# Turning a unit's running maxima head by head: two places in a two-slot PSUM ring, and two VectorE row-maximum operations

## The chip, the cores and the metric

One core of one Trainium2 chip runs the whole program. The metric is the device time of one execution in microseconds (us). The kernel before takes 1535.57 us, the median of two runs (1534.63 and 1536.50).

## What is computed

The reference takes 8 graphs of 1500 nodes with 64 features, and one 0/1 adjacency matrix per graph. Each graph goes through a masked graph attention with 4 heads (16 features in and out per head), then three propagations over the same adjacency, and after each of the four a residual and a layer norm over the features:

```
masked = a * scores
masked = where(masked >= 0, masked, 0.2 * masked) / sqrt(16)
attn   = softmax(masked + (-1e9 where a == 0)) * (a != 0)
x = layernorm(x + relu(attn @ feats + bias))
x = layernorm(x + (adj + I) @ x / rowsum(adj + I))
x = layernorm(x + (adj @ (x @ w2) + bias2))
x = layernorm(x + where(adj @ x > 0.5, 1, 0 * (adj @ x)))
```

## The kernel before, in words

The attention is cut into 48 **units**: 8 graphs, 2 pairs of heads, 3 slices of 500 nodes. A unit has 12 **steps**, and a step q (0 to 575) handles 125 neighbours against the slice's 500 nodes for both heads of the pair. So a graph is 72 steps, and a step's place in its graph is r = q mod 72. The other three layers of the graph before are spread over the same steps.

What a step passes through:

- TensorE fills Z (`fill_z`, L599 and L601): for each of the two heads one matmul with the mask and one with the scores. Z is a ring with two slots (RZ = 2), each of two PSUM banks of 500 columns, one for each head.
- ScalarE empties the slot with a leaky ReLU into a row buffer LS (`bend`, L774), 126x1000 in one operation.
- VectorE folds the row into the running maxima RP (`maximum`, L914 and L920), and in the unit's last step writes them to RUN (L918).
- Once the unit is folded, TensorE turns RUN into a ring slot (`turn_run`, L612, 8 transposes, 4 for each head), VectorE reduces the slot to the maxima of each node (`row_maxima`, L926, LMAX), SyncE writes LMAX to memory and reads it back broadcast to all partitions as MB (`spread_maxima`, L413 and L419).
- 19 steps after its fill, GpSimd (two of three rows, L533) or VectorE (every third, L934) subtracts MB from the row; 21 steps after it ScalarE takes the exponential (`expo`, L782), and 23 steps after it TensorE weighs the features with it (`weigh`, L628, for two steps together).
- At the unit's end the sums are turned into a ring slot as well (`turn_sums`, L637, and `keep`, L948 to L960).

The other layers use a bank M1 for their products (`collect`, L683), a ring slot for turning them back (`turn_back`, L697), and VectorE, ScalarE and GpSimd for adding, squares, powers and scaling (L983 to L1024, L828, L832, L538, L542). `power` and `low` on GpSimd are written for HALVES parts in the changed kernel; with HALVES = 1 they do what they did.

The order on every engine is written out by hand. Each engine runs its own loop over q, and tables say in which steps of a unit or a graph something stands: TURNED for turning the maxima on TensorE, MAXIMA for reducing them on VectorE, SPREAD for SyncE. For the six units of a graph TURNED puts the turning at r = 15, 27, 38, 51, 63 and 75 (the last is r = 3 of the next graph), behind the fill of that step. I call these the **six places**; they are units 24 to 29 in the fifth graph, for instance. The turning of the last unit stands at LAST_RT = 576.

Who may use a ring slot when is set by a list, `ring`, of everything that goes through Z in order. `ring_free` looks at the entry two before: a fill must have been bent, a turning reduced (`max_found`), a turned sum kept, a turned-back layer added. With one entry for the turning, the entries around it and their waits are

```
Z(q)   RT(u)              Z(q+1)          Z(q+2)
       waits bend(q-1)    waits bend(q)   waits max_found of u
```

Of the kernel before, what the change touches and what calls it, by code (L numbers as in the profile page):

```python
# [6 lines left out]
B, N, F = 8, 1500, 64  # L7
H, D = 4, 16
P = 125
# [33 lines left out]
POOL_AT, SUB_AT, EXP_AT, WEIGH_AT = 19, 19, 21, 23  # L43
LAG = POOL_AT

TURNED = (15, 15, 14, 15, 15, 15)
MAXIMA = (15, 15, 14, 14, 15, 14)
SPREAD = (16, 16, 16, 15, 15, 15)
TAKE = (35, 35, 35, 34, 34, 34)
SUMS = (36, 36, 36, 36, 35, 35)  # L50
# [2 lines left out]
CENTRE = (25, 45, 67, 86)  # L53
SQUARE = (26, 47, 66, 87)
SUM = (26, 46, 66, 88)
POWER = (28, 49, 66, 89)
SCALE = (28, 49, 67, 90)
HIGH = (29, 51, 69)
LOW = (30, 50, 70)
# [12 lines left out]
FEATURES = (14, 18, 19, 20, 22, 23, 27, 30, 32)  # L72
TAKEN = (14, 18, 19, 20, 22, 24, 27, 30, 32)
LOWER = (17, 23, 29)
KINDS = tuple((kind, c) for c in range(NS) for kind in ("XT", "FT", "FE"))
LOWER_KINDS = tuple(("FT", c) for c in range(NS))
LOADS = (57, 55, 60, 59, 65, 62, 66, 68, 30, 35, 37, 38)
# [23 lines left out]
def adj_resnorm(nc, x, adj, wv, wself, wother, bias0, w2, bias2, out):  # L101
# [13 lines left out]
    with ctx:  # L115
# [197 lines left out]
        for q in range(END):  # L313
            if q < QN:
                ring.append(("Z", q))
            if rows_at(q, BACK):
                ring.append(("W", *rows_at(q, BACK)))
            if turned_at(q, TURNED, LAST_RT) is not None:
                ring.append(("RT", turned_at(q, TURNED, LAST_RT)))
            if unit_at(q, SUMS) is not None:  # L320
                ring.append(("G", unit_at(q, SUMS)))
# [41 lines left out]
        def _(sp):  # L363
# [40 lines left out]
                             ).then_inc(at_in[slot], 16)  # L404

            def spread_maxima(u):
                sp.wait_ge(max_found, u + 1)
                if u >= 2:

                    sp.wait_ge(mb_in[u % 2], 16 * (u // 2))  # L410

                for rows in (slice(0, 112), slice(112, P)):
                    sp.dma_start(spread[u % 2].rearrange("(h i c) -> i h c", i=P, c=ST)[rows],  # L413
                                 LMAX[rows, u % 2, :].rearrange("p (h c) -> p h c", c=ST)).then_inc(max_out[u % 2], 16)
                sp.wait_ge(max_out[u % 2], 32 * (u // 2 + 1))
# [52 lines left out]
        def _(pool):  # L468
# [66 lines left out]
            def power(b, l):  # L535

                pool.wait_ge(var_ok, 4 * b + l + 1)
                nc.gpsimd.tensor_tensor(RSTD[:, :], RSTD[:, :], NHALF[:, :], ALU.pow).then_inc(rstd_ok, 1)  # L538

            def low(b, l):  # L540
                pool.wait_ge(xh_ready, 3 * b + l + 1)
                nc.gpsimd.tensor_tensor(XP[:, :, F:2 * F], X[:, :, :], XP[:, :, 0:F], ALU.subtract).then_inc(xp_ready, 1)  # L542

            for q in range(END):
                if layer_at(q, LOW):
                    low(*layer_at(q, LOW))
                if layer_at(q, POWER):
                    power(*layer_at(q, POWER))
# [17 lines left out]
        def _(pe):  # L566
            def ring_free(n):

                if n < RZ:
                    return  # L570
                kind, *at = ring[n - RZ]
                if kind == "Z":
                    pe.wait_ge(bent, at[0] + 1)
                elif kind == "RT":
                    pe.wait_ge(max_found, at[0] + 1)
                elif kind == "G":
                    pe.wait_ge(kept_seq, 5 * at[0] + 5)
                else:
                    b, l, c = at
                    pe.wait_ge(added, 9 * b + 3 * l + c + 1)  # L580
# [21 lines left out]
                                            FS[:, p, s * C:(s + 1) * C], start=False, stop=True)  # L602
                last.then_inc(z_full, 1)

            def turn_run(u):

                pe.wait_ge(maxed, STEPS * (u + 1))
                ring_free(place["RT", u])
                z = banks("RT", u)
                for hh in range(2):  # L610
                    for c in range(ST):
                        last = nc.tensor.transpose(z[:P, hh, c * P:(c + 1) * P], RUN[:, u % 2, hh, c:C:ST], ID[:P, :P])  # L612
                last.then_inc(run_turned, 1)

            def weigh(w):
# [62 lines left out]
            def collect(b, l, c, part):  # L678
                if part == 0:
                    m1_free(order["Y", b, l, c])  # L680
                    pe.wait_ge(xp_ready, 3 * b + l + 1)
# [39 lines left out]
            for q in range(END):  # L721
# [11 lines left out]
                e = q - WEIGH_AT  # L733
                if 0 <= e < QN and e % 2:
                    weigh(e // 2)
                u = turned_at(q, TURNED, LAST_RT)
                if u is not None:
                    turn_run(u)


            pe.wait_ge(kept_seq, 5 * NU)
# [151 lines left out]
        def _(dve):  # L893
# [13 lines left out]
            def maximum(q):  # L907
# [5 lines left out]
                if m == 0:  # L913
                    nc.vector.tensor_scalar(run, rows, FLOOR, None, ALU.max).then_inc(maxed, 1)  # L914
                elif m == STEPS - 1:
                    if u >= 2:
                        dve.wait_ge(run_turned, u - 1)
                    nc.vector.tensor_tensor(RUN[:, u % 2, :, :], rows, run, ALU.max).then_inc(maxed, 1)  # L918
                else:
                    nc.vector.tensor_tensor(run, rows, run, ALU.max).then_inc(maxed, 1)  # L920

            def row_maxima(u):
                dve.wait_ge(run_turned, u + 1)
                if u >= 2:
                    dve.wait_ge(max_out[u % 2], 32 * (u // 2))
                nc.vector.tensor_reduce(LMAX[:, u % 2, :].rearrange("p (h c) -> p h c", c=ST),  # L926
                                        banks("RT", u)[:P].rearrange("p h (c m) -> p h c m", c=ST),
                                        AX.X, ALU.max).then_inc(max_found, 1)

            def subtract(e):  # L930
# [65 lines left out]
            def scale(b, l):  # L996

                dve.wait_ge(m1_read, order["S", b, l])
                dve.wait_ge(rstd_ok, 4 * b + l + 1)
# [108 lines left out]
            for q in range(END):  # L1108
# [7 lines left out]
                u = turned_at(q, MAXIMA, LAST_RT)  # L1116
                if u is not None:
                    row_maxima(u)
# [69 lines left out]
```

## Time and profile before

| | |
|---|---|
| median of two runs | 1535.57 us |
| the profiled execution | 1531.98 us, of which the span of the core's instructions is 1529.9 us |
| TensorE busy | 1343.7 us, 88% of the span |
| VectorE busy | 1266.8 us, 83% |
| ScalarE busy | 1223.3 us, 80% |
| GpSimd busy | 1035.5 us, 68% |
| mean granted TensorE clock | 0.946 of full speed |

Columns of the rows below: a group of instructions is "line engine operation out<-in (shape) xcount", its busy time and the mean ns of one, and then the engine's idle time just before them with what ended most of it. In a timeline a row is "start, us it takes, engine line operation xcount", and square brackets tell the idle time before it and what ended it. A row of a timeline may cover several instructions in a row, and the start of the next can lie before its end, since operations are pipelined. PE is TensorE, PEld its weight loads, DVE VectorE, ACT ScalarE, POOL GpSimd and SP SyncE.

### The profile page before, as it was taken

Reading aid. Unit: us, or ns where it says so; the run is one execution under the profiler, and the core shown is the slowest. Engines: PE = TensorE matmul, PEld = TensorE weight load, DVE = VectorE, ACT = ScalarE, POOL = GpSimd, SP = SyncE. Lnnn points to the kernel's source line nnn. Section 1 sums busy time; section 2 is a strip of 40 time slices with the busy share of each in tenths; the row PEclk is TensorE's granted clock in tenths of the full one; section 3 lists DMA queues with packets and bytes.
Section 4 is the critical chain, followed back from the end, with each engine's and each line's share of the span. In section 5 each row is a group of like instructions: output and inputs, shape, how many; then the busy total and the mean of one; then the engine's idle time right before and its main releaser. Section 6 shows DMA issues by size and latency. Waiting matters only on the chain. (4 is left out here: it accounts for less than half of the span.)

```text
span 1529.9 us, 21041 instructions
## 1 busy us (share of the span) xinstructions
PE 1343.7 (88%) x7296; PEld 675.7 (44%) x7296; DVE 1266.8 (83%) x1490; ACT 1223.3 (80%) x1404; POOL 1035.5 (68%) x562
## 2 busy tenths in 40 slices
PE   2788889998989988999989989999889999899856
PEld 1443334544445544444545544454445444355323
DVE  2677998897888889898888889988898988988864
ACT  1587888887988878898888878988788888888731
POOL 3067777787677776778677776778767776867412
PEclk7898999999999999999999999999999999999978
DMA  6624552434424442425325344245424343200000
GB/s 94 111 34 63 61 79 52 68 41 48 90 43 63 57 65 56 54 61 52 72 62 75 34 49 89 45 60 59 66 62 58 53 47 69 54 15 16 26 10 11
DMA packets 140879, 84.95 MB, mean 56 GB/s; under 512 B 100372, under 2 KB 130522, under 8 KB 140762
## 3 DMA queue, kind: packets, MB, share of 16 engines
q1 hardware_dynamic: 125542, 64.67, 20.1%
q0 software_dynamic: 14160, 18.51, 15.6%
q8 instruction: 58, 0.95, 0.3%
q10 hardware_dynamic: 1072, 0.43, 0.1%
q14 instruction: 47, 0.39, 0.1%
HBM read 103.33 MB, written 21.38 MB: 82 GB/s over the span
## 5 line engine op out<-in xcount | busy, mean ns | idle before, releaser
L533 POOL TENSOR_TENSOR LS<-LS,MB 125x1000 f32<-125x1000 f32 x372 | 860.7, 2332 | 368.2 <-DVE LS L934 272.2
L774 ACT ACTIVATE LS<-Z 126x1000 f32<-126x1000 f32 x576 | 575.1, 1000 | 150.6 <-PE Z L601 149.9
L782 ACT ACTIVATE LS<-LS 125x1000 f32<-125x1000 f32 x576 | 595.8, 1035 | 47.3 <-POOL LS L533 22.5
L920 DVE TENSOR_TENSOR RP<-LS,RP 125x1000 f32<-125x1000 f32 x480 | 575.6, 1199 | 45.0 <-ACT LS L774 19.4
L599 PE MATMUL Z<-AT,BI 126*126 126x500 fp8e4 x1152 | 367.2, 401 | 77.8 <-ACT LS L774 44.2
L601 PE MATMUL Z<-FS,FO 128*125 128x500 f16 x1152 | 348.8, 384 | 0.0
L628 PE MATMUL M<-LS,V 126*18 126x500 f32 x2304 | 315.9, 622 | 8.8 <-ACT LS L782 8.7
L934 DVE TENSOR_TENSOR LS<-LS,MB 125x1000 f32<-125x1000 f32 x204 | 319.9, 1573 | 0.1
L599 PEld LDWEIGHTS Z<-AT,BI 126*126 126x126 bf16 x1152 | 126.8, 138 | 376.6 <-issue 158.2
L683 PE MATMUL M<-AT,XP 125*128 125x500 fp8e4 x756 | 203.4, 378 | 3.6 <-ACTq L821 3.1
L601 PEld LDWEIGHTS Z<-FS,FO 128*125 128x125 f16 x1152 | 162.0, 141 | 92.4 <-issue 9.2
L926 DVE TENSOR_REDUCE LMAX<-Z 125x8 f32<-125x1000 f32 x48 | 57.5, 1199 | 73.8 <-PE Z L612 73.6
L683 PEld LDWEIGHTS M<-AT,XP 125*128 125x128 f16 x756 | 72.8, 101 | 83.0 <-ACTq L821 10.3
L612 PE MATMUL Z<-ID,RUN 125*125 125x125 f32 x384 | 95.4, 392 | 9.8 <-ACT LS L774 9.5
L612 PEld LDWEIGHTS Z<-ID,RUN 125*125 125x125 f32 x384 | 91.6, 322 | 25.5 <-issue 11.8
L538 POOL TENSOR_TENSOR RSTD<-RSTD,NHALF 125x12 f32<-125x12 f32 x28 | 70.4, 2516 | 32.3 <-DVE RSTD L994 30.5
L628 PEld LDWEIGHTS M<-LS,V 126*18 126x18 f32 x2304 | 39.1, 97 | 111.5 <-issue 64.2
L637 PE MATMUL Z<-E,O 128*125 128x36 f32 x384 | 55.4, 294 | 32.4 <-ACT O L788 21.2
L914 DVE TENSOR_SCALAR RP<-LS 125x1000 f32<-125x1000 f32 x48 | 57.4, 1197 | 30.1 <-ACT LS L774 29.2
L637 PEld LDWEIGHTS Z<-E,O 128*125 128x125 f32 x384 | 50.8, 206 | 54.6 <-ACT O L788 40.4
L481 POOL DMA_DIRECT2D adj_cast<-in_adj_dram x96 | 52.9, 553 | 30.7 <-DMA AT<-adj_cast 30.7
L697 PEld LDWEIGHTS Z<-WW,YT 128*125 128x125 f32 x504 | 63.7, 188 | 12.9 <-issue 7.2
(133 smaller groups left out, 798.7 us busy)
## 6 DMA issues: line engine op xcount, KB each, us to landing
MB<-row_maxima SPq DMA_DIRECT2D x48, 500.0 KB, 4.1
adj_cast<-in_adj_dram POOLq DMA_DIRECT2D x96, 183.1 KB, 4.5
FO<-PARTS SPq DMA_DIRECT2D x120, 46.9 KB, 2.1
FS<-PARTS SPq DMA_DIRECT2D x120, 46.9 KB, 2.1
XF<-in_x_dram SPq DMA_DIRECT2D x8, 336.0 KB
XA<-in_x_dram SPq DMA_DIRECT2D x8, 336.0 KB
out_dram<-X SPq DMA_DIRECT2D x7, 375.0 KB
AT<-adj_cast SPq DMA_TRANSPOSE x144, 2.8
```

The lines of the kernel that those rows point to most:

```text
L533: nc.gpsimd.tensor_tensor(rows, rows, MB[:P, u % 2, :, :], ALU.subtract).then_inc(sub_pool, 1)
L538: nc.gpsimd.tensor_tensor(RSTD[:, :], RSTD[:, :], NHALF[:, :], ALU.pow).then_inc(rstd_ok, 1)
L599: nc.tensor.matmul(z[:PD, hh, :], BI[:, :], AT[:P + 1, g % RS, pair, PAD:CP, k], start=True, stop=False)
L601: last = nc.tensor.matmul(z[:P, hh, :], FO[:, 2 * p + hh, m * P:(m + 1) * P], FS[:, p, s * C:(s + 1) * C], start=False, stop=True)
L612: last = nc.tensor.transpose(z[:P, hh, c * P:(c + 1) * P], RUN[:, u % 2, hh, c:C:ST], ID[:P, :P])
L628: last = nc.tensor.matmul(M0[VW * n:VW * n + VC, 0:C], V[:, b % 2, e % STEPS, 2 * p + hh, :], LS[:PD, e % RL, hh, :], start=(j == 0), stop ...
L637: last = nc.tensor.matmul(z[:P, 0, k * 2 * VC:(k + 1) * 2 * VC], O4[:, k * P:(k + 1) * P], E[:, :, :].rearrange("p h o -> p (h o)"), start ...
L683: last = nc.tensor.matmul(M1[:, 0:C], XP[:, m, :], AT[:P, (NS * b + c) % RS, m // KK, PAD:CP, m % KK], start=(m == 0), stop=(m == NT - 1 a ...
L774: nc.scalar.activation(LS[:PD, q % RL, :, :], banks("Z", q)[:PD], ACT.Prelu, alpha=SLOPE).then_inc(bent, 1)
L782: nc.scalar.activation(rows, rows, ACT.Exp, scale=0.25).then_inc(exps, 1)
L920: nc.vector.tensor_tensor(run, rows, run, ALU.max).then_inc(maxed, 1)
L934: nc.vector.tensor_tensor(rows, rows, MB[:P, u % 2, :, :], ALU.subtract).then_inc(sub_dve, 1)
```

## The change

The turning of a unit becomes two ring entries, ("RT", u, 0) and ("RT", u, 1), directly behind one another. Each takes a whole slot of two banks but uses only its own head's bank. `turn_run(u, h)` turns 4 blocks, `row_maxima(u, h)` reduces 125x500 to 125x4, and `max_found` counts two for a unit. TURNED and MAXIMA have the same steps for both heads. Only the last unit's second head stands a step later (`LAST_RT + h`). SyncE waits for both heads before it writes LMAX. In the list, "G" is now entered before "W" in a step; no step has both.

```diff
-TURNED = (15, 15, 14, 15, 15, 15)
-MAXIMA = (15, 15, 14, 14, 15, 14)
+TURNED = ((15, 15, 14, 15, 15, 15), (15, 15, 14, 15, 15, 15))
+MAXIMA = ((15, 15, 14, 14, 15, 14), (15, 15, 14, 14, 15, 14))
...
-            if turned_at(q, TURNED, LAST_RT) is not None:
-                ring.append(("RT", turned_at(q, TURNED, LAST_RT)))
...
+            for h in range(2):
+                if turned_at(q, TURNED[h], LAST_RT + h) is not None:
+                    ring.append(("RT", turned_at(q, TURNED[h], LAST_RT + h), h))
...
-                sp.wait_ge(max_found, u + 1)
+                sp.wait_ge(max_found, 2 * (u + 1))
...
-                    pe.wait_ge(max_found, at[0] + 1)
+                    pe.wait_ge(max_found, 2 * at[0] + at[1] + 1)
...
-            def turn_run(u):
+            def turn_run(u, h):
 
                 pe.wait_ge(maxed, STEPS * (u + 1))
-                ring_free(place["RT", u])
-                z = banks("RT", u)
-                for hh in range(2):
-                    for c in range(ST):
-                        last = nc.tensor.transpose(z[:P, hh, c * P:(c + 1) * P], RUN[:, u % 2, hh, c:C:ST], ID[:P, :P])
+                ring_free(place["RT", u, h])
+                z = banks("RT", u, h)
+                for c in range(ST):
+                    last = nc.tensor.transpose(z[:P, h, c * P:(c + 1) * P], RUN[:, u % 2, h, c:C:ST], ID[:P, :P])
                 last.then_inc(run_turned, 1)
...
-            def row_maxima(u):
-                dve.wait_ge(run_turned, u + 1)
+            def row_maxima(u, h):
+                dve.wait_ge(run_turned, 2 * u + h + 1)
...
-                nc.vector.tensor_reduce(LMAX[:, u % 2, :].rearrange("p (h c) -> p h c", c=ST),
-                                        banks("RT", u)[:P].rearrange("p h (c m) -> p h c m", c=ST),
+                nc.vector.tensor_reduce(LMAX[:, u % 2, ST * h:ST * (h + 1)],
+                                        banks("RT", u, h)[:P, h, :].rearrange("p (c m) -> p c m", c=ST),
```

How the waits move shows in the order of instructions. TensorE at the first of the six places of the fifth graph (r = 15, unit 24): the fill of step 303, the turning, the fill of step 304, a weighing, of the kernel before:

```order
L601 MATMUL Z<-FS,FO 125x500 x2
L612 MATMUL Z<-ID,RUN 125x125 [waits bent,maxed]
L612 MATMUL Z<-ID,RUN 125x125 x7
L599 MATMUL Z<-AT,BI 126x500 [waits bent]
L599 MATMUL Z<-AT,BI 126x500
L601 MATMUL Z<-FS,FO 125x500 x2
L628 MATMUL M<-LS,V 18x500 [waits exps]
```

and of the changed kernel:

```order
L607 MATMUL Z<-FS,FO 125x500 x2
L617 MATMUL Z<-ID,RUN 125x125 [waits bent,maxed]
L617 MATMUL Z<-ID,RUN 125x125 x3
L617 MATMUL Z<-ID,RUN 125x125 [waits bent,maxed]
L617 MATMUL Z<-ID,RUN 125x125 x3
L605 MATMUL Z<-AT,BI 126x500 [waits max_found]
L605 MATMUL Z<-AT,BI 126x500
L607 MATMUL Z<-FS,FO 125x500 x2
L633 MATMUL M<-LS,V 18x500 [waits exps]
```

The wait for bend(q), which stood ahead of the fill of step q + 1, now stands ahead of the second four transposes, and the fill waits for the first head's maxima.

VectorE at the end of the program (steps 576 and 577, unit 47): the last fold into RUN, the row maxima, the keeping of unit 45's sums, subtractions, of the kernel before:

```order
L918 TENSOR_TENSOR RUN<-LS,RP 125x1000 [waits run_turned,maxed,bent]
L926 TENSOR_REDUCE LMAX<-Z 125x8 [waits max_out1,run_turned]
L949 TENSOR_SCALAR RSUM<-Z 125x8 [waits o4_turned]
L951 RECIPROCAL RSUM<-RSUM 125x8 [waits kept_seq]
L953 TENSOR_TENSOR Z<-Z,RSUM 125x8x16 [waits kept_seq]
L956 TENSOR_TENSOR Z<-Z,B 125x8x16 [waits kept_seq]
L960 SCALAR_TENSOR_TENSOR XA<-Z,XA 125x4x32 [waits kept_seq]
L934 TENSOR_TENSOR LS<-LS,MB 125x1000 [waits mb_in0] x5
```

and of the changed kernel:

```order
L925 TENSOR_TENSOR RUN<-LS,RP 125x1000 [waits run_turned,maxed,bent]
L933 TENSOR_REDUCE LMAX<-Z 125x4 [waits max_out1,run_turned]
L956 TENSOR_SCALAR RSUM<-Z 125x8 [waits o4_turned]
L958 RECIPROCAL RSUM<-RSUM 125x8 [waits kept_seq]
L960 TENSOR_TENSOR Z<-Z,RSUM 125x8x16 [waits kept_seq]
L963 TENSOR_TENSOR Z<-Z,B 125x8x16 [waits kept_seq]
L967 SCALAR_TENSOR_TENSOR XA<-Z,XA 125x4x32 [waits kept_seq]
L941 TENSOR_TENSOR LS<-LS,MB 125x1000 [waits mb_in0]
L933 TENSOR_REDUCE LMAX<-Z 125x4 [waits max_out1,run_turned]
L941 TENSOR_TENSOR LS<-LS,MB 125x1000 [waits mb_in0] x4
```

Here the second head's reduction has moved behind the keeping and one subtraction.

## Rows read from the trace of the kernel before

**Rows 1.** The page's busy times by engine.

```profile
PE 1343.7 (88%) x7296; PEld 675.7 (44%) x7296; DVE 1266.8 (83%) x1490; ACT 1223.3 (80%) x1404; POOL 1035.5 (68%) x562
```

**Rows 2.** Waits of the whole span: who for whom, us, times, longest.

```profile
ACT LS L774 <- PE Z L601: 149.9, 166, 19.1
...
PEld Z L599 <- DVE LMAX L926: 15.6, 23, 0.9
```

**Rows 3.** The page's group of the row maxima.

```profile
L926 DVE TENSOR_REDUCE LMAX<-Z 125x8 f32<-125x1000 f32 x48 | 57.5, 1199 | 73.8 <-PE Z L612 73.6
```

**Rows 4.** VectorE's groups by form: a half-size operation from PSUM.

```profile
L965 DVE TENSOR_TENSOR PARTS<-M,PARTS 128x500 f16<-128x500 f32 x21 | 14.2, 677 | 17.8 <-ACT PARTS L813 17.8
```

**Rows 5.** Timeline at r = 15 (unit 24), 760 to 766 us.

```profile
760.96 1.89 PE L612 MATMUL Z<-ID,RUN 125*125 125x125 f32 x8
...
762.07 0.98 ACT L774 ACTIVATE LS<-Z 126x1000 f32<-126x1000 f32 x1
...
763.11 0.64 PE L599 MATMUL Z<-AT,BI 126*126 126x500 fp8e4 x2 [0.26 <-ACT LS L774]
...
764.01 1.19 DVE L934 TENSOR_TENSOR LS<-LS,MB 125x1000 f32<-125x1000 f32 x1
```

**Rows 6.** Timeline at r = 27 (unit 25), 791 to 798 us.

```profile
791.74 2.06 PE L612 MATMUL Z<-ID,RUN 125*125 125x125 f32 x8 [1.54 <-ACT LS L774]
...
792.42 0.99 ACT L774 ACTIVATE LS<-Z 126x1000 f32<-126x1000 f32 x1
...
793.64 0.79 PE L599 MATMUL Z<-AT,BI 126*126 126x500 fp8e4 x2
793.85 1.20 DVE L926 TENSOR_REDUCE LMAX<-Z 125x8 f32<-125x1000 f32 x1 [0.72 <-PE Z L612]
```

**Rows 7.** Timeline at r = 51 (unit 27), 848 to 854 us.

```profile
848.16 2.07 PE L612 MATMUL Z<-ID,RUN 125*125 125x125 f32 x8 [0.21 <-ACT LS L774]
...
849.57 1.00 ACT L774 ACTIVATE LS<-Z 126x1000 f32<-126x1000 f32 x1
...
850.63 1.19 DVE L926 TENSOR_REDUCE LMAX<-Z 125x8 f32<-125x1000 f32 x1
```

**Rows 8.** Timeline at r = 75 (unit 29), 909 to 917 us.

```profile
910.56 0.99 ACT L774 ACTIVATE LS<-Z 126x1000 f32<-126x1000 f32 x1
...
911.60 0.64 PE L599 MATMUL Z<-AT,BI 126*126 126x500 fp8e4 x2 [1.00 <-ACT LS L774]
```

**Rows 9.** Timeline at r = 38 (unit 26), 818 to 824 us.

```profile
818.23 1.00 ACT L774 ACTIVATE LS<-Z 126x1000 f32<-126x1000 f32 x1 [0.37 <-PE Z L601]
...
819.72 2.09 PE L612 MATMUL Z<-ID,RUN 125*125 125x125 f32 x8
...
821.65 0.59 PE L599 MATMUL Z<-AT,BI 126*126 126x500 fp8e4 x2
821.85 1.20 DVE L926 TENSOR_REDUCE LMAX<-Z 125x8 f32<-125x1000 f32 x1 [2.07 <-PE Z L612]
```

**Rows 10.** Timeline at r = 63 (unit 28), 878 to 884 us.

```profile
878.06 1.01 ACT L774 ACTIVATE LS<-Z 126x1000 f32<-126x1000 f32 x1 [0.66 <-PE Z L601]
878.50 1.89 PE L612 MATMUL Z<-ID,RUN 125*125 125x125 f32 x8
...
880.42 1.20 DVE L926 TENSOR_REDUCE LMAX<-Z 125x8 f32<-125x1000 f32 x1 [2.70 <-PE Z L612]
...
881.53 1.19 DVE L934 TENSOR_TENSOR LS<-LS,MB 125x1000 f32<-125x1000 f32 x1
```

**Rows 11.** VectorE's timeline at the end, 1430 to 1442 us.

```profile
1434.22 1.20 DVE L926 TENSOR_REDUCE LMAX<-Z 125x8 f32<-125x1000 f32 x1 [2.61 <-PE Z L612]
...
1436.64 5.63 DVE L934 TENSOR_TENSOR LS<-LS,MB 125x1000 f32<-125x1000 f32 x5
```

**Rows 12.** Stretches: busy by engine, then PEclk (granted clock), DMA share, GB/s.

```profile
794.00:796.00 2.00, 2.00 (x8) 0.43 (x10) 2.00 (x2) 1.73 (x2) 0.36 (x1) 0.50 0.04 1
796.00:798.00 2.00, 2.00 (x12) 0.70 (x5) 1.75 (x4) 1.98 (x3) 1.77 (x1) 0.67 0.26 17
```

More of the change, by code:

```diff
@@ L55 @@
 SUM = (26, 46, 66, 88)
-POWER = (28, 49, 66, 89)
 SCALE = (28, 49, 67, 90)
 HIGH = (29, 51, 69)
-LOW = (30, 50, 70)
 COLLECT = ((33, 34, 35, 36, 37, 38, 39, 40, 41, 42, 43, 44),
@@ L74 @@
 LOWER = (17, 23, 29)
+HALVES = 1
+POWERS = ((28, 49, 66, 89),)
+LOWS = ((30, 50, 70),)
 KINDS = tuple((kind, c) for c in range(NS) for kind in ("XT", "FT", "FE"))
@@ L315, in adj_resnorm @@
                 ring.append(("Z", q))
+            if unit_at(q, SUMS) is not None:
+                ring.append(("G", unit_at(q, SUMS)))
             if rows_at(q, BACK):
                 ring.append(("W", *rows_at(q, BACK)))
-            if turned_at(q, TURNED, LAST_RT) is not None:
-                ring.append(("RT", turned_at(q, TURNED, LAST_RT)))
-            if unit_at(q, SUMS) is not None:
-                ring.append(("G", unit_at(q, SUMS)))
+            for h in range(2):
+                if turned_at(q, TURNED[h], LAST_RT + h) is not None:
+                    ring.append(("RT", turned_at(q, TURNED[h], LAST_RT + h), h))
             if feature_at(q, FEATURES, KINDS):
@@ L533, in subtract, with power, low @@
                 nc.gpsimd.tensor_tensor(rows, rows, MB[:P, u % 2, :, :], ALU.subtract).then_inc(sub_pool, 1)
-            def power(b, l):
+            def power(b, l, k):
+                part = RSTD[:, NT // HALVES * k:NT // HALVES * (k + 1)]
                 pool.wait_ge(var_ok, 4 * b + l + 1)
-                nc.gpsimd.tensor_tensor(RSTD[:, :], RSTD[:, :], NHALF[:, :], ALU.pow).then_inc(rstd_ok, 1)
-            def low(b, l):
+                nc.gpsimd.tensor_tensor(part, part, NHALF[:, 0:NT // HALVES], ALU.pow).then_inc(rstd_ok, 1)
+            def low(b, l, k):
+                tiles = slice(NT // HALVES * k, NT // HALVES * (k + 1))
                 pool.wait_ge(xh_ready, 3 * b + l + 1)
-                nc.gpsimd.tensor_tensor(XP[:, :, F:2 * F], X[:, :, :], XP[:, :, 0:F], ALU.subtract).then_inc(xp_ready, 1)
+                nc.gpsimd.tensor_tensor(XP[:, tiles, F:2 * F], X[:, tiles, :], XP[:, tiles, 0:F], ALU.subtract).then_inc(xp_ready, 1)
             for q in range(END):
[L545 to L548, printed above, removed]
+                for k in range(HALVES):
+                    if layer_at(q, LOWS[k]):
+                        low(*layer_at(q, LOWS[k]), k)
+                for k in range(HALVES):
+                    if layer_at(q, POWERS[k]):
+                        power(*layer_at(q, POWERS[k]), k)
                 e = q - POOL_AT
@@ L680, in collect @@
                     m1_free(order["Y", b, l, c])
-                    pe.wait_ge(xp_ready, 3 * b + l + 1)
+                if part * HALVES % CUTS == 0:
+                    pe.wait_ge(xp_ready, HALVES * (3 * b + l) + part * HALVES // CUTS + 1)
                 for m in range(NT // CUTS * part, NT // CUTS * (part + 1)):
@@ L735, in _ @@
                     weigh(e // 2)
-                u = turned_at(q, TURNED, LAST_RT)
-                if u is not None:
-                    turn_run(u)
+                for h in range(2):
+                    u = turned_at(q, TURNED[h], LAST_RT + h)
+                    if u is not None:
+                        turn_run(u, h)
             pe.wait_ge(kept_seq, 5 * NU)
@@ L916, in maximum @@
                     if u >= 2:
-                        dve.wait_ge(run_turned, u - 1)
+                        dve.wait_ge(run_turned, 2 * (u - 1))
                     nc.vector.tensor_tensor(RUN[:, u % 2, :, :], rows, run, ALU.max).then_inc(maxed, 1)
@@ L998, in scale @@
                 dve.wait_ge(m1_read, order["S", b, l])
-                dve.wait_ge(rstd_ok, 4 * b + l + 1)
+                dve.wait_ge(rstd_ok, HALVES * (4 * b + l + 1))
                 nc.vector.tensor_copy(M1[:P, 0:NT], RSTD[:, :]).then_inc(factors_in, 1)
@@ L1115, in _ @@
                     add_squares(*layer_at(q, SUM))
-                u = turned_at(q, MAXIMA, LAST_RT)
-                if u is not None:
-                    row_maxima(u)
+                for h in range(2):
+                    u = turned_at(q, MAXIMA[h], LAST_RT + h)
+                    if u is not None:
+                        row_maxima(u, h)
                 at = feature_at(q, LOWER, LOWER_KINDS)
```

## The prediction

> **What bounds the kernel now.** I read the busy times first [rows 1]. TensorE is busy 88% of the span, VectorE 83%, ScalarE 80%, GpSimd 68%. No engine is full, so what a microsecond is worth depends on who waits for whom at that place. Next come the waits [rows 2]: ScalarE waits 149.9 us in total for TensorE to fill Z, while the fills lose only 15.6 us to the row maxima. The slot that the turned maxima hold is thus no big obstacle. The row maxima themselves are 48 operations of 1199 ns, and VectorE stands idle 73.8 us ahead of them, nearly all of it until TensorE has turned RUN [rows 3]. That idle time is the prize for handing over the first head sooner.
>
> Then I read the timeline at the six places of the fifth graph. The question at each is whether bend(q), ScalarE's emptying of the fill just ahead of the turning, has ended when half of the eight transposes are done. Before, only the fill of step q + 1 needed that, and it comes behind all eight. Now the second four need it.
>
> **The change part by part.**
>
> *TensorE's work.* The same eight transposes, in two calls. At r = 38 the next fill starts 1.93 us after the turning starts (819.72 to 821.65), so four take about 0.95 us [rows 9]. Nothing is added but the wait.
>
> *VectorE's work.* One reduction of 1.20 us becomes two. The trace has no such half. The nearest row is a 128x500 operation from PSUM, 0.68 us [rows 4]. The next operation starts 1.11 us after a 1.20 us reduction (880.42 to 881.53), so 0.09 us of each lies beside its follower [rows 10], and the pair takes 2 x 0.68 - 0.09 = 1.27 us, or 0.07 us more. With 48 units that is 3.4 us of busy time. It lies in VectorE's idle time where VectorE waits for the turning, so I cost it within the places below. If that cover were gone, it would be the whole 3.4 us. The bounds of the pair are 1.20 us, if a half took half, and 1.36 us, if nothing overlapped. The overlap of 0.09 us is what the row shows. The Trainium skill ("VectorE: DVE Perf Modes", section "The DRAIN you can't avoid") says that a VectorE operation doesn't start until the pipe of the one before is empty. By that the pair would take 1.36 us, and 48 of them 7.7 us more. The follower's start here speaks against it.
>
> *The moved wait.* The second four transposes wait for bend(q), and behind them on TensorE stand the fill of q + 1 and all that follows. The fill waits in addition for the first head's maxima. These are ready 0.68 us after the first four end, while the second four take 0.95 us, so that wait is hidden wherever VectorE is free. It costs the rest where VectorE isn't: at most one 1.19 us operation.
>
> Place by place (the times are those of the fifth graph):
>
> - r = 15: bend ends at 762.07 + 0.98 = 763.05, and the fill starts at 763.11. The first four are done near 761.9, so the second four now start after 763.05 and the fill about 0.95 + 0.05 = 1.0 us later than before. VectorE's subtraction at 764.01 follows the reduction and moves alike, so all engines move: +1.0 [rows 5].
> - r = 27: bend ends at 793.41, and the fill started at 793.64, so it moves by 0.95 + 0.05 - 0.23 = 0.8. VectorE's reduction ended at 795.05; the second half would end near 793.41 + 1.15 + 0.68 = 795.24, +0.2. The place costs between these, and I take the middle: +0.5 [rows 6].
> - r = 38: bend ended at 819.23, before the turning began at 819.72. No new wait, and TensorE goes straight on, so its chain stays. VectorE ends its maxima (0.68 us after the last transpose, not 1.20) 0.5 us sooner. I take 0, since ScalarE is there fed by TensorE. The bounds are -0.6 and +0.1 [rows 9].
> - r = 51: bend ends at 850.57; the fill moves by 1.0. The reduction ended at 851.82 and now ends at 850.57 + 1.15 + 0.68 = 852.4, +0.6. I take +0.75 [rows 7].
> - r = 63: bend ends at 879.07, and the first four end near 879.45, so there is no new wait. The subtraction at 881.53 comes 0.5 us sooner; VectorE had idled 2.70 us before the maxima, so this one is a gain where GpSimd and VectorE lead. I take -0.3, between 0 and -0.55 [rows 10].
> - r = 75: bend ends at 911.55, and TensorE already stood idle 1.00 us for it before the fill at 911.60. The idle time moves half a turning forward, and the four transposes come behind it: +1.0 [rows 8]. VectorE's maxima move by up to 1.75 us. I count 1.05, because the fills lead.
>
> A graph thus costs 1.0 + 0.5 + 0 + 0.75 - 0.3 + 1.05 = 3.0 us. Seven graphs have this pattern, except that the last unit of the last one stands apart: 7 x 3.0 - 1.05 = 19.95. In the first graph there are no other layers beside the attention and the bends are less late; I give it three quarters, 2.2 us, an estimate from the six values above, with bounds of 1 and 3.6.
>
> *The end.* Unit 47's first head no longer waits for the whole turning. VectorE idled 2.61 us before the reduction at 1434.22, which now starts about 1 us sooner, and the keeping and the first subtraction of the run at 1436.64 follow at once [rows 11]. The second head stands behind that subtraction, and TensorE's second four behind the keeping. I take -0.7, with bounds of -1 and +1.
>
> The sum: 19.95 + 2.2 - 0.7 = 21.45 us. The profiled execution took 1531.98 us, which gives 1553.4. The median of the runs is 3.6 us above it, so on the median's scale it is 1535.57 + 21.45 = **1557.0 us**. With the lower bound at each place (0.95, 0.2, -0.6, 0.6, -0.55, 0.95) the sum is 1.55 a graph and about 10 us in all; with the upper (1.05, 0.85, 0.1, 1.0, 0, 1.75) it is 4.75 a graph and about 36 us. That is 1546 to 1571.
>
> **The rivals.**
>
> *The delays vanish in slack: 1536 to 1543, value 1539.* No engine is over 88% busy [rows 1], and ScalarE idles 149.9 us for fills in places that could be others than these [rows 2]. If at each place another chain arrived later anyway, only VectorE's 3.4 us would be left. Against it: at r = 15 both the fill and the subtraction directly follow the waited-for event [rows 5], so no second chain is visible.
>
> *The freed slot wins: faster, about 1519.* The second head's slot is free 0.5 us sooner, and the first head's reduction runs beside the second's transposes. If the fills that lost 15.6 us to the maxima [rows 2] got it back and bend(q) were mostly done in time, the kernel would be faster by up to about 16.5 us (with 0.9 us more for waits of the matmul rather than of the weights, an estimate). It decides where bend(q) ends before the fourth transpose. That is so at r = 38 and 63, but not at the other four [rows 5 to 8]. So it needs ScalarE to run about 1 us ahead of where this trace has it.
>
> *The clock falls once more per graph: about 1569.* At r = 27 TensorE idles 1.54 us before the turning [rows 6], and from about 794 us its granted clock is 0.50 of full, the 1.2 GHz level, and on average 0.67 in the next 2 us [rows 12]. The fill's first two matmuls then take 0.79 us instead of 0.64. At r = 75 the new idle time before the second four is 1.9 us, as long as that one. If low stretches of such length (2 us at 0.50 and two thirds of 2 us more, 3.3 us, in which up to half is lost, 1.7 us) come there too, that is 7 x 1.7 = 12 us on top: 1569. For it speaks the likeness of the idle times; against it that idle times of 1.00 us at r = 75 now cause nothing there. The Trainium skill ("TensorE: Matmul & The Clock Gate", section "A second HAM failure mode: psum-queue depth-cycling") says that short idle times between groups of matmuls, from cycling through PSUM banks, are enough to make the clock fall and rise again. By that the clock would fall at r = 75 too; the rows bear it out at r = 27 alone so far, hence the 0.15 below.
>
> **How the numbers follow.** The forecast (10 to 36 us slower) has 0.62, the vanished delays 0.15, the freed slot 0.08, the clock 0.15. A measurement here tells about 2% (30.7 us, that is 1504.9 or 1566.3) from no change. Faster by over 2% lies beyond even the freed slot's 1519: 0.02. Slower by over 2% is most of the clock's case (0.11) and the upper end of the forecast (0.06): 0.17. The rest, 0.81, is within 2%. The range of 1541 to 1573 leaves out the freed slot, most of the vanished delays and the worst of the clock, about 0.2.
>
> **What would show it.** In the changed profile TensorE's second transposes should wait for ScalarE's bend about 1.2 us at r = 15 and 51 and 1.9 us at r = 75, a new line among the waits of some 4 us a graph, 30 us in all. The fills should follow four transposes directly, with hardly a wait for the maxima. VectorE's halves should take 0.68 us. At r = 38 and 63 its following operations should come 0.5 us sooner. The forecast is wrong if ScalarE's waits for fills don't grow, if the shifts of one place are gone at the next, or if the number of low-clock stretches changes.

## The result and the profile after

The changed kernel takes 1578.94 us (two runs, 1578.60 and 1579.28) against 1535.57 us: a ratio of 1.0294, with a 95% interval of 1.0273 to 1.0314. It is 43.4 us slower, twice the forecast of 21.4 us and above its range.

The page of the changed kernel, busy times and then the two groups that answer to [rows 1] and [rows 3] and to ScalarE's bend:

```profile
span 1576.8 us, 21183 instructions
...
PE 1373.1 (87%) x7296; PEld 691.2 (44%) x7296; DVE 1253.1 (79%) x1538; ACT 1222.3 (78%) x1404; POOL 1036.2 (66%) x562
...
L781 ACT ACTIVATE LS<-Z 126x1000 f32<-126x1000 f32 x576 | 575.7, 1001 | 199.1 <-PE Z L607 198.3
...
L933 DVE TENSOR_REDUCE LMAX<-Z 125x4 f32<-125x500 f32 x96 | 65.0, 677 | 88.2 <-PE Z L617 88.0
```

ScalarE's and GpSimd's work is what it was, spread over a longer span. A half reduction takes 677 ns, as forecast. But VectorE idles 88.2 us before the row maxima instead of 73.8, so the prize wasn't won, and ScalarE waits 198.3 us for fills where it waited 149.9 [rows 2]. TensorE's busy time has grown by 29 us though it has the same 7296 matmuls: its instructions take longer. That is the first sign of a lower clock; the mean granted clock of the profiled execution is 0.933 of full speed, and it was 0.946.

The waits of the changed kernel (who for whom, us, times, longest):

```profile
POOL LS L535 <- DVE LS L941: 298.6, 135, 6.6
ACT LS L781 <- PE Z L607: 198.3, 189, 16.0
...
PE Z L617 <- ACT LS L781: 44.5, 41, 3.4
...
PEld Z L617 <- DVE RP L927: 31.5, 24, 3.8
```

The third row shown is the new wait, transposes for a bend, 44.5 us (it was 9.5). No row for a fill that waits for the maxima is near the top.

At r = 75 of the fifth graph the timeline now reads as follows; it answers to [rows 8]:

```profile
928.23 0.97 PE L617 MATMUL Z<-ID,RUN 125*125 125x125 f32 x4
929.24 0.68 DVE L933 TENSOR_REDUCE LMAX<-Z 125x4 f32<-125x500 f32 x1 [1.90 <-PE Z L617]
930.07 0.99 ACT L781 ACTIVATE LS<-Z 126x1000 f32<-126x1000 f32 x1
...
931.20 1.15 PE L617 MATMUL Z<-ID,RUN 125*125 125x125 f32 x4 [2.00 <-ACT LS L781]
...
932.19 0.59 PE L605 MATMUL Z<-AT,BI 126*126 126x500 fp8e4 x2
932.39 0.68 DVE L933 TENSOR_REDUCE LMAX<-Z 125x4 f32<-125x500 f32 x1 [2.48 <-PE Z L617]
```

Four transposes, 2.00 us of nothing, four transposes 0.14 us behind the bend's end, and the fill 1.13 us behind that end, where it was 0.05 us. That is the forecast's picture. From the second graph on, the second four wait 1.25 to 1.7 us at r = 15 and 1.40 us at r = 51 (seven units each), and 2.00 us at r = 75 (six units, the last one being split in another way). At r = 27 they wait 0.6 to 0.7 us, which the forecast's list of new waits left out.

At r = 51, [rows 7] before, something is added:

```profile
865.88 1.15 PE L617 MATMUL Z<-ID,RUN 125*125 125x125 f32 x4 [0.20 <-ACT LS L781]
...
868.43 1.25 PE L617 MATMUL Z<-ID,RUN 125*125 125x125 f32 x4 [1.40 <-ACT LS L781]
...
869.48 1.04 PE L605 MATMUL Z<-AT,BI 126*126 126x500 fp8e4 x2
...
870.31 1.04 PE L607 MATMUL Z<-FS,FO 128*125 128x500 f16 x2
...
871.39 1.00 ACT L781 ACTIVATE LS<-Z 126x1000 f32<-126x1000 f32 x1 [2.17 <-PE Z L607]
```

The fill's pairs take 1.04 us each, not 0.64 and 0.59, and ScalarE gets its fill 3.10 us after the bend's end at 868.29. Before, it was 1.15 us after the end at 850.57:

```profile
851.72 1.00 ACT L774 ACTIVATE LS<-Z 126x1000 f32<-126x1000 f32 x1 [0.22 <-PE Z L601]
```

The stretches of the same place show why (busy by engine, then granted clock, DMA share, GB/s):

```profile
866.00:868.00 2.00, 1.03 (x4) 0.84 (x4) 1.90 (x2) 2.00 (x3) 1.57 (x2) 1.00 0.00 0
868.30:870.30 2.00, 1.86 (x6) 1.53 (x7) 1.30 (x3) 0.92 (x1) 2.00 (x2) 0.50 0.00 0
870.30:872.30 2.00, 2.00 (x11) 0.39 (x9) 2.00 (x3) 0.91 (x2) 1.07 (x1) 0.69 0.07 2
```

TensorE is half idle for 2 us, and then its granted clock is 0.50, the 1.2 GHz level. In the kernel before, no low stretch begins at this place in any graph. From 200 to 1400 us the clock record holds 15 low stretches with 61 us in all before, and 26 with 112 us after. (A low stretch is one in which the granted clock is 0.50.)

The new ones are not spread evenly. At the wait of 1.40 us at r = 51, or within 2 us behind it, a low stretch begins in all seven graphs from the second on; before, none did. At the longer wait of 2.00 us at r = 75 one begins in two of six; before, none did. At the turning at r = 27 four of the seven graphs had one before; now all seven have one, and three of these last twice as long (6.8 us, not 3.4).

**Where the 43 us arise.** I took the start of bend at each multiple of 12 steps in both traces; the growth of the difference between two of them belongs to the turning that lies between. The table has the mean of six or seven graphs (the second on), in us, for the changed kernel and for the experiments below. All are held against the one trace of the kernel before, so a chance loss in that trace shows as a gain in all the others; the profiled runs of e2 and e4 were the slowest of their four. The first graph is not in the table.

| place r | forecast | changed | e1 | e2 | e4 | e8 |
|---|---|---|---|---|---|---|
| 75 | 1.05 | 1.22 | 0.43 | 1.92 | 0.88 | 7.10 |
| 15 | 1.0 | 1.62 | 0.02 | 2.21 | 1.12 | 1.11 |
| 27 | 0.5 | 0.89 | -0.52 | 0.84 | 0.55 | 0.16 |
| 38 | 0 | 0.04 | -0.02 | -0.02 | 0.04 | -0.13 |
| 51 | 0.75 | 1.96 | -0.13 | 2.01 | 0.47 | 1.37 |
| 63 | -0.3 | 0.06 | -0.01 | 0.00 | 0.06 | 0.14 |
| a graph | 3.0 | 5.8 | -0.2 | 7.0 | 3.1 | 9.8 |

The difference is 41.1 us at step 564, and 46.9 us at the end of the span (1576.8 - 1529.9), so the last 12 steps and the end give 5.8 us more.

### The profile page after: what moved, and what is told of

Read it like the earlier page. It is cut to its first block and busy times, and to the rows that moved or that the text cites. A ratio compares the mean times of both kernels' runs of the same rounds, so it can differ in the third digit from the quotient of the medians.

```text
span 1576.8 us, 21183 instructions
## 1 busy us (share of the span) xinstructions
PE 1373.1 (87%) x7296; PEld 691.2 (44%) x7296; DVE 1253.1 (79%) x1538; ACT 1222.3 (78%) x1404; POOL 1036.2 (66%) x562
## 5 line engine op out<-in xcount | busy, mean ns | idle before, releaser
L781 ACT ACTIVATE LS<-Z 126x1000 f32<-126x1000 f32 x576 | 575.7, 1001 | 199.1 <-PE Z L607 198.3
L605 PE MATMUL Z<-AT,BI 126*126 126x500 fp8e4 x1152 | 372.8, 406 | 57.6 <-ACT LS L781 29.2
L607 PE MATMUL Z<-FS,FO 128*125 128x500 f16 x1152 | 354.2, 389 | 0.0
L633 PE MATMUL M<-LS,V 126*18 126x500 f32 x2304 | 320.5, 630 | 8.3 <-ACT LS L789 8.3
L941 DVE TENSOR_TENSOR LS<-LS,MB 125x1000 f32<-125x1000 f32 x204 | 302.0, 1485 | 0.1
L689 PE MATMUL M<-AT,XP 125*128 125x500 fp8e4 x756 | 206.9, 383 | 1.1 <-ACTq L828 0.7
L617 PE MATMUL Z<-ID,RUN 125*125 125x125 f32 x384 | 104.8, 406 | 54.8 <-ACT LS L781 44.5
L933 DVE TENSOR_REDUCE LMAX<-Z 125x4 f32<-125x500 f32 x96 | 65.0, 677 | 88.2 <-PE Z L617 88.0
L617 PEld LDWEIGHTS Z<-ID,RUN 125*125 125x125 f32 x384 | 94.0, 321 | 77.7 <-issue 38.7
L689 PEld LDWEIGHTS M<-AT,XP 125*128 125x128 f16 x756 | 74.2, 102 | 83.2 <-issue 10.2
## 6 DMA issues: line engine op xcount, KB each, us to landing
FO<-PARTS SPq DMA_DIRECT2D x120, 46.9 KB, 2.1
FS<-PARTS SPq DMA_DIRECT2D x120, 46.9 KB, 2.1
```

The costliest lines, as they stand in the source:

```text
L605: nc.tensor.matmul(z[:PD, hh, :], BI[:, :], AT[:P + 1, g % RS, pair, PAD:CP, k], start=True, stop=False)
L607: last = nc.tensor.matmul(z[:P, hh, :], FO[:, 2 * p + hh, m * P:(m + 1) * P], FS[:, p, s * C:(s + 1) * C], start=False, stop=True)
L617: last = nc.tensor.transpose(z[:P, h, c * P:(c + 1) * P], RUN[:, u % 2, h, c:C:ST], ID[:P, :P])
L633: last = nc.tensor.matmul(M0[VW * n:VW * n + VC, 0:C], V[:, b % 2, e % STEPS, 2 * p + hh, :], LS[:PD, e % RL, hh, :], start=(j == 0), stop ...
L781: nc.scalar.activation(LS[:PD, q % RL, :, :], banks("Z", q)[:PD], ACT.Prelu, alpha=SLOPE).then_inc(bent, 1)
L941: nc.vector.tensor_tensor(rows, rows, MB[:P, u % 2, :, :], ALU.subtract).then_inc(sub_dve, 1)
```

## The experiments

The runs were made on several chips. Where two kernels of different groups are compared, the ratios to the kernel before, which ran beside each group, are the fairer measure.

**VectorE's split alone** (e1). One ring entry and one slot as before:

```diff
-                for hh in range(2):
-                    for c in range(ST):
-                        last = nc.tensor.transpose(...)
-                last.then_inc(run_turned, 1)
+                for hh in range(2):
+                    for c in range(ST):
+                        last = nc.tensor.transpose(...)
+                    last.then_inc(run_turned, 1)
```

and `row_maxima` reduces each head behind its own count.

> The kernel before with VectorE's row maxima taken head by head, each as soon as its four transposes are done; one ring entry and one turning as before. Theory A (the moved wait costs, the two reductions don't): 1530 to 1539 us, no change within 0.3%, VectorE's halves 0.68 us each. Rival B (the smaller VectorE operations cost by themselves): at least 10 us slower than before.

Measured: 1529.91 us against 1533.33 us of the kernel before on the same chip, a ratio of 0.9968 (0.9951 to 0.9984). The group of the maxima, to be held against [rows 3]:

```profile
L927 DVE TENSOR_REDUCE LMAX<-Z 125x4 f32<-125x500 f32 x96 | 63.7, 676 | 51.3 <-PE Z L612 50.9
```

VectorE idles 22.5 us less before its maxima, but works 6.2 us more on them, and of the rest little reaches the path: -0.5 us at r = 27, nothing elsewhere. The two small operations are not what costs. (The interval is just clear of 1, and the time just under the expected range; e10 repeats the run.)

**The split, and the wait** (e2).

```diff
                 for hh in range(2):
+                    if hh and u < NU - 1:
+                        pe.wait_ge(bent, STEPS * u + TURNED[u % UPG] + 1)
                     for c in range(ST):
```

> As e1_split_only, but the second head's four transposes wait for bend(q), still in one slot and one ring entry; the last unit doesn't wait. Theory A (the wait for bend(q) ahead of the second four transposes is the whole loss, but for the end): 1570 to 1576 us, 36 to 41 us slower than before, with the same new stretches of low clock as in the changed kernel. Rival B (the ring's order, with fills that wait for the maxima, costs by itself): under 1560 us.

Measured: 1577.15 us, ratio 1.0274 (1.0235 to 1.0313). One wait, and the kernel is as slow as the changed one, with a single ring entry and no fill that waits for the maxima. The expected range ended at 1576. From 200 to 1400 us it has 28 low stretches with 119 us. So the wait is the cause. The fair partner for the second entry is e3 below, which like e2 leaves the last unit whole: 1.0261 (1.0246 to 1.0277). The two don't differ by more than their intervals, so the second entry costs nothing beyond the wait that could be seen here; a few us either way would not be seen.

**The last unit whole** (e3). The changed kernel, in which unit 47 has one ring entry and both heads at step 576:

```diff
-                if turned_at(q, TURNED[h], LAST_RT + h) is not None:
+                if turned_at(q, TURNED[h], LAST_RT + h) is not None and (q < LAST_RT or not h):
                     ring.append(("RT", turned_at(q, TURNED[h], LAST_RT + h), h))
...
-                for c in range(ST):
-                    last = nc.tensor.transpose(z[:P, h, c * P:(c + 1) * P], RUN[:, u % 2, h, c:C:ST], ID[:P, :P])
-                last.then_inc(run_turned, 1)
+                for hh in range(h, 2 if u == NU - 1 else h + 1):
+                    for c in range(ST):
+                        last = nc.tensor.transpose(z[:P, hh, c * P:(c + 1) * P], RUN[:, u % 2, hh, c:C:ST], ID[:P, :P])
+                    last.then_inc(run_turned, 1)
```

> The changed kernel with the last unit turned and reduced in one ring entry, as before. The difference between the two traces grows by 5.8 us from step 564 to the end. Theory A (that comes from the last unit's second head standing a step later and waiting for the kept sums): 1573 to 1575 us, 4 to 6 us faster than the changed kernel. Rival B (it comes from a long stretch of low clock at the end): 1577 to 1580 us, as the changed kernel.

Measured: 1575.17 us, ratio 1.0261 (1.0246 to 1.0277), 3.8 us below the changed kernel; by the ratios it is 5 us, but the two intervals just touch (1.0273 to 1.0314 for the changed kernel). From step 564 to the end the difference from the kernel before grows by 1.9 us (from 41.0 to 42.9), not 5.8. The changed kernel's TensorE at that place:

```profile
1472.81 1.28 PE L617 MATMUL Z<-ID,RUN 125*125 125x125 f32 x4 [2.08 <-DVE RUN L925]
1473.88 1.46 PE L689 MATMUL M<-AT,XP 125*128 125x500 fp8e4 x3
1476.25 1.25 PE L617 MATMUL Z<-ID,RUN 125*125 125x125 f32 x4 [0.91 <-DVE XA L967]
```

The second head waits for the kept sums (L967), and behind it stand the layers' products and turnings, for which VectorE then waits:

```profile
1478.13 4.52 DVE L941 TENSOR_TENSOR LS<-LS,MB 125x1000 f32<-125x1000 f32 x4
1485.68 0.43 DVE L1031 SCALAR_TENSOR_TENSOR Y<-Z,X 125x256 f32<-125x256 f32 x1 [3.02 <-PE Z L703]
```

That is Theory A's picture, but the clock has a part in it too (Rival B). Three of the layers' products take 1.46 us here (L689); in the kernel before three of them take 0.81 us, at 1436.34 us and full clock. Stretches of the changed kernel and then of the kernel before, each from before the last unit's turning on:

```profile
1471.00:1481.00 10.00, 7.28 (x24) 3.05 (x25) 8.07 (x13) 2.07 (x2) 2.69 (x2) 0.50 0.02 2
1481.00:1491.00 10.00, 9.28 (x38) 3.48 (x37) 6.98 (x8) 6.26 (x7) 0.00 (x0) 0.58 0.19 51
...
1428.00:1438.00 10.00, 9.28 (x45) 4.23 (x46) 7.06 (x11) 3.74 (x5) 4.56 (x2) 0.83 0.01 0
1438.00:1448.00 10.00, 9.14 (x65) 3.92 (x64) 10.00 (x10) 8.55 (x9) 0.00 (x0) 1.00 0.22 54
```

The low stretch at the last unit's turning lasts 20.5 us in the changed kernel and 3.4 us in the kernel before. Over all traces, what is lost from step 564 on goes with its length: -0.1 to 0.2 us where it is 3.4 us long (e1, e8, e11), 1.9 to 3.0 us at 6.8 or 10.2 us (e2, e3, e5, e6, e9, e10), and 4.9 to 5.8 us at 13.7 or 20.5 us (the changed kernel, e4, e7). The last three are the ones with the late second head, so the head and the clock come together here, and no run keeps them apart. In all three the stretch begins before the last unit's turning does.

**Fillers** (e4). TensorE gets something to do while it waits. A slot has two banks and a head uses one; the fillers write the other one, which nobody reads.

```diff
+                if h and u < NU - 1:
+                    spare = banks("RT", u, 0)
+                    for _n in range((4, 2, 0, 5, 0, 8)[u % UPG]):
+                        nc.tensor.matmul(spare[:P, 1, :], ID16[:, :], ID16[:, :].unsqueeze(1).to_broadcast([P, ST, P]),
+                                         start=True, stop=True)
                 ring_free(place["RT", u, h])
```

> The changed kernel with 4, 2, 0, 5, 0 and 8 matmuls of 500 columns (at r = 15, 27, 38, 51, 63, 75) between the first and the second four transposes, into the unused bank of the first head's slot, their results never read. They keep TensorE at work while it waits for bend(q). Theory A (about half of the loss is the clock, which falls after these idle times): the low stretches between 200 and 1400 us fall from 26 to about 15, and the time to 1558 to 1566 us. Rival B (the clock is no part of it): 1579 to 1583 us.

Measured: 1554.90 us, ratio 1.0128 (1.0105 to 1.0152). That is 24 us less than the changed kernel (25 us by the ratios), for 144 matmuls more, and below both ranges: the clock's part was larger than the half that I had expected. TensorE at r = 51, with five fillers (L617) between the halves (L622):

```profile
859.27 1.15 PE L622 MATMUL Z<-ID,RUN 125*125 125x125 f32 x4 [0.21 <-ACT LS L786]
860.26 1.23 PE L617 MATMUL Z<-ID 125*125 125x500 f16 x5
861.73 1.18 PE L622 MATMUL Z<-ID,RUN 125*125 125x125 f32 x4 [0.25 <-ACT LS L786]
862.75 0.59 PE L605 MATMUL Z<-AT,BI 126*126 126x500 fp8e4 x2
```

The second half still begins only behind the bend (860.67 + 1.00 = 861.67), so the moved wait is all there. What has gone is the clock's fall:

```profile
859.60:861.60 2.00, 1.88 (x9) 1.21 (x8) 1.90 (x2) 2.00 (x4) 1.56 (x2) 1.00 0.00 0
861.60:863.60 2.00, 1.87 (x8) 1.43 (x8) 1.46 (x4) 1.00 (x2) 2.00 (x2) 1.00 0.00 0
```

From 200 to 1400 us it has 14 low stretches with 61 us, as many microseconds as the kernel before, and none at the waits at r = 51 and 75. The changed kernel has 51 us of low clock more. At half speed they cost at most about 25 us, an estimate that takes TensorE as busy throughout. A graph loses 3.1 us, where I had forecast 3.0.

**A quarter of the fillers** (e7).

```diff
-                    for _n in range((4, 2, 0, 5, 0, 8)[u % UPG]):
+                    for _n in range((1, 1, 0, 1, 0, 2)[u % UPG]):
```

> As e4_fillers with 1, 1, 0, 1, 0 and 2 fillers instead of 4, 2, 0, 5, 0 and 8, about a quarter. Theory A (the fillers help because they keep TensorE from standing idle, and so the clock up): in between, 1560 to 1576 us, with more low stretches than the 14 of e4_fillers. Rival B (something else in e4_fillers helps, such as weights loaded earlier): 1555 us, as e4_fillers.

Measured: 1571.66 us (runs from 1562.45 to 1575.97), ratio 1.0230 (1.0189 to 1.0271), in between, with 92 us of low clock from 200 to 1400 us. So the fillers help by their number, as work in the idle time, not by being there.

**The wait where the bend has ended** (e5), at r = 38 and 63 alone. Against e2:

```diff
-                    if hh and u < NU - 1:
+                    if hh and u < NU - 1 and u % UPG in (2, 4):
```

> As e1_split_only, with the wait for bend(q) ahead of the second head's transposes at r = 38 and 63 alone, where bend(q) has ended by then. Theory A (a moved wait costs only where bend ends later than the fourth transpose): as e1_split_only, 1528 to 1533 us. Rival B (the wait breaks TensorE's stream wherever it stands): 2 places x 8 graphs x 1 us, about 1546 us.

Measured: 1531.45 us, ratio 0.9991 (0.9974 to 1.0008). A wait that is met before it is reached costs nothing that could be seen here.

**The wait at r = 51 alone** (e6). Against e5:

```diff
-                    if hh and u < NU - 1 and u % UPG in (2, 4):
+                    if hh and u < NU - 1 and u % UPG in (3,):
```

> As e1_split_only, with the wait at r = 51 alone (8 units). Theory A (delay of about 0.6 us plus a stretch of low clock behind it, about 2.0 us a unit in the traces): 1544 to 1548 us, with some 6 to 8 more low stretches between 200 and 1400 us than the 11 of e1_split_only. Rival B (the delay alone): 1534 to 1537 us.

Measured: 1542.12 us, ratio 1.0037 (1.0010 to 1.0064). Both theories missed. Against e5, which ran beside it on the same chip, it is 10.7 us slower. The ten runs are not one cluster: three lie at 1530.25 to 1533.33 us with a mean granted clock of 0.955 to 0.963, six at 1542.05 to 1545.64 with 0.942 to 0.952, and one at 1537.70. So the same wait doesn't bring the clock down equally often in every run.

The profiled run is the one between, so its trace doesn't show what the six slower ones did. In it five of seven graphs lose 0.6 to 0.7 us there, one gains 0.5, and one loses 2.2, which is the size of the loss with a fall of the clock; a low stretch begins behind the wait in that graph alone. (e4's trace gains the same 0.5 in the same graph, so that is a loss of the one trace of the kernel before.) In e2 and in the changed kernel six and five of the seven graphs lose 2.0 us or more at this place, and a low stretch begins behind the wait in all seven; there the other places have their waits too. Why that decides I didn't find out.

**The second head a step later** (e8), a fill between the two heads, the last unit whole:

```diff
-TURNED = ((15, 15, 14, 15, 15, 15), (15, 15, 14, 15, 15, 15))
-MAXIMA = ((15, 15, 14, 14, 15, 14), (15, 15, 14, 14, 15, 14))
+TURNED = ((15, 15, 14, 15, 15, 15), (16, 16, 15, 16, 16, 16))
+MAXIMA = ((15, 15, 14, 14, 15, 14), (16, 16, 15, 15, 16, 15))
```

> The two ring entries with the second head's turning and maxima one step later (a fill between the two), and the last unit turned whole. Theory A (two ring places cost nothing once no bend is waited for early): 1525 to 1538 us, TensorE's waits for bend ahead of the transposes back to about 10 us. Rival B (the ring's second entry costs by itself): over 1545 us.

Measured: 1611.22 us, ratio 1.0497 (1.0458 to 1.0537), the slowest of all, against my theory. The table shows that r = 75 alone costs 7.1 us a graph. Its timeline at r = 75 of the fifth graph, whose steps already lie in the sixth:

```profile
961.42 1.18 PE L618 MATMUL Z<-ID,RUN 125*125 125x125 f32 x4
962.64 0.68 DVE L934 TENSOR_REDUCE LMAX<-Z 125x4 f32<-125x500 f32 x1 [4.71 <-PE Z L618]
...
965.45 0.42 DVE L1032 SCALAR_TENSOR_TENSOR Y<-Z,X 125x256 f32<-125x256 f32 x1
965.92 1.09 PE L605 MATMUL Z<-AT,BI 126*126 126x500 fp8e4 x2 [3.32 <-DVE Y L1032]
...
967.88 1.00 ACT L782 ACTIVATE LS<-Z 126x1000 f32<-126x1000 f32 x1 [6.84 <-PE Z L607]
```

Here a layer's rows are turned back through the ring too. With the second head behind them, the next fill's slot is that of these rows, and it waits for VectorE to add them. VectorE in turn stood 4.71 us for the second head. A fill, which feeds ScalarE, has come to wait for two others' work.

**The same but at r = 75** (e9), where both heads stand together as in the changed kernel. Against e8:

```diff
-TURNED = ((15, 15, 14, 15, 15, 15), (16, 16, 15, 16, 16, 16))
-MAXIMA = ((15, 15, 14, 14, 15, 14), (16, 16, 15, 15, 16, 15))
+TURNED = ((15, 15, 14, 15, 15, 15), (16, 16, 15, 16, 16, 15))
+MAXIMA = ((15, 15, 14, 14, 15, 14), (16, 16, 15, 15, 16, 14))
```

> As e8_second_later, but at r = 75 both heads stand directly behind one another, as in the changed kernel. Theory A (nearly all that e8_second_later loses is lost at r = 75, where its fill of the next step waits for the layer row that was turned back just before; 7.1 us a graph there against 1.2 in the changed kernel): 8 x 5.9 = 47 us less than its 1611, 1558 to 1570 us. Rival B (a head turned a step later costs about the same at all six places): 1598 to 1606 us.

Measured: 1585.71 us, ratio 1.0326 (1.0290 to 1.0363). That is 26 us less than e8, not the 47 us expected: r = 75 now costs 2.4 us a graph, not 1.2, and from 200 to 1400 us there are 136 us of low clock, more than in any other kernel here. Neither theory's number holds. Putting the two heads together again at r = 75 gives back a third of e8's loss of 77.5 us. In both kernels the first graph, which the table leaves out, has lost 9.9 and 7.6 us by step 72, against 0.5 us in the changed kernel. Where the rest goes stays open.

**e1 once more, with more runs** (e10); the kernel and its diff are e1's.

> e1_split_only again, with more rounds: VectorE's two reductions in one ring entry. Theory A (it is faster than the kernel before by half a microsecond a unit at r = 27 alone, about 5 us): ratio 0.995 to 0.999. Rival B (no difference; the first ratio was chance): an interval around 1.000.

Measured: 1532.60 us against 1534.93 us, ratio 0.9988 (0.9971 to 1.0004). The first interval was clear of 1 and this one isn't. The split alone is worth 0.3% at best and isn't shown to be faster. Its gain at r = 27 does come back in four traces (-0.5, -0.6, -0.5 and -0.5 us a graph in e1, e5, e6 and e10).

**Fillers and the last unit whole** (e11), e3's diff and e4's together.

> e4_fillers and e3_last_whole together: fillers while TensorE waits, and the last unit in one ring entry. Theory A (clock and end are separate terms and add up): 1549 to 1554 us, 4 us faster than e4_fillers. Rival B (the end's loss is the clock's as well, and the fillers have it already): 1554 to 1558 us.

Measured: 1558.71 us, ratio 1.0157 (1.0127 to 1.0187). Both theories' ranges ended at or below 1558, and the kernel is not faster than e4, whose ratio was 1.0128 (1.0105 to 1.0152). In the profiles the span is shorter, 1553.8 against 1557.3 us, but the profiled run of e11 is the fastest of its four and that of e4 the slowest. From step 564 on the difference grows by 0.1 us in e11 and by 5.2 us in e4, while the low stretch there lasts 3.4 and 13.7 us. So the traces show that the end behaves otherwise with the late head than without it, the medians don't show a gain, and how much of the end's loss is the clock's stays open. A graph costs 3.2 us in e11, which confirms e4's 3.1.

## Why the prediction was wrong

**The direction and the mechanism were right.** The wait for bend(q) moved ahead of the second four transposes, and e2 shows that it alone makes the loss. The transposes wait 1.25, 1.40 and 2.00 us at r = 15, 51 and 75, where I had said 1.2 and 1.9; from the second graph on they don't wait at r = 38 and 63.

**The sum of the places came out, in part by luck.** With the clock held up by fillers a graph costs 3.1 us (e4) or 3.2 us (e11), not 3.0. The single terms were off by up to 0.36 us, and the worst of them was r = 63. There I took -0.3 for VectorE's earlier subtraction, and nothing of it reached the path (0.06). r = 51 was 0.28 us too high, and the two nearly cancel. The first graph, up to step 84, costs 0.1 us in e4 and 1.7 in e11, where I had 2.2; the steps from there to 564 cost 22.2 us in both, where I had 19.95. That e4's median is 1554.9 us, beside my 1557.0, is luck as well: the forecast had -0.7 us at the end, where e4's trace has +5.2. The gain of the split lies at r = 27, in e1.

**The step that failed is the clock.** The sum has no term for it. I had it as a rival of its own with 0.15, at one place (r = 75), worth 12 us: "the clock falls once more per graph: about 1569". It falls at several places, and not chiefly where I had looked for it: at the wait at r = 51 in seven graphs of seven, at r = 75 in two of six, and at r = 27 in seven where it was four. There are 11 low stretches more and 51 us of low clock more between 200 and 1400 us, and e4 prices them at 24 us by the medians. My own sign of being wrong, that the number of low stretches changes, has come. My argument against it was that an idle time of 1.00 us at r = 75 did nothing before. But the new idle times are longer, 1.25 to 2.00 us, and at three places of six, and I held only the longest of them against r = 27. What decides whether the clock falls behind one of them isn't shown; it isn't the length of the wait alone, since in this trace 2.00 us brought it down less often than 1.40. I should have asked it of each lengthened idle time, and put the clock into the sum rather than beside it. The section of the Trainium skill that I cited, "A second HAM failure mode: psum-queue depth-cycling" ("TensorE: Matmul & The Clock Gate"), says that short idle times from cycling through PSUM banks suffice. The trace agrees, with 26 low stretches for 15, and the rule should have weighed more.

**The end was mis-signed.** I had -0.7 us, since VectorE's first reduction starts sooner. It is +5.8 us from step 564 on, of which about 4 us go in e3's trace. I had looked at VectorE's row alone. The second head stands in TensorE's in-order stream behind the wait for the kept sums, and the layers' products behind it were late for ScalarE and VectorE. They also ran at half clock for 20.5 us, and the two causes aren't kept apart.

In the spans of three profiles the loss divides as follows. Up to step 564, e4 is 22.2 us behind the kernel before (the places had been forecast at 19.95 + 2.2 = 22.15); its end adds 5.2 us (1557.3 - 1529.9 = 27.4 in all); and the changed kernel, without fillers, has 19.5 us more (1576.8 - 1557.3). That makes 46.9. The profiled run of e4 was the slowest of its four (1559.09 us, median 1554.90), so this division makes the fillers' part too small: by the medians it is 24 us.

**The other rivals.** The delays did not vanish in slack. The freed slot did not win either: e1 has the earlier hand-over of the first head without the moved wait, and is at most 0.3% faster.

## What to carry to other kernels

When a ring entry is split in two, look at what the second part's slot waits for: a wait that stood ahead of the next fill now stands ahead of more work on the same in-order engine, and in these runs it was free only where it was met before it was reached. A reduction can be split without splitting the ring entry, since its consumer may start on the bank that is done. Where a change lengthens TensorE's idle times at several places, give the clock a term in the sum, with bounds, for each of them. Matmuls into an unused bank during the waits tell how much of a loss is the clock's. A trace is one run: see where it lies among the runs of its kernel before two traces are compared.

## What the runs showed of the hardware that I had not expected

144 matmuls whose results nobody reads made the kernel 24 us faster, from 1578.94 to 1554.90 us. With them no low stretch begins any more at the waits of 1.40 and 2.00 us at r = 51 and 75, which they fill but for some 0.2 us. A quarter as many gave 7 us. A wait of the same length doesn't bring the clock down each time: 2.00 us at r = 75 did in two graphs of six, and in e2 1.91 us there did in all six; 1.40 us at r = 51 did in all seven. With the wait at r = 51 alone (e6, 1.31 us) the clock fell there in one graph of seven of the profiled run, and with the same 1.31 us beside the other waits (e2) in all seven. The runs of e6 spread over 15 us (1530.25 to 1545.64), the slower ones at a lower mean granted clock.
